# A transformer layer in fp32 on one core: the total of squares by one-column products

## The chip, the cores and the metric

The kernel runs on one core of a Trainium2 chip. The metric is the device time of one execution in microseconds (us), as the median of several runs. Before the change it is 652.82 us (three runs, 652.47 to 654.33).

## The reference

The input is x, 8 x 1024 tokens of 256 channels. First comes an attention block without a score matrix (softmax of q over the head's 16 channels, softmax of k over the tokens, state = kᵀv), with a residual and a layer norm. Then comes the feed-forward block, which is where the change lies:

```
h = layer_norm(x, ln1_g, ln1_b)
h = h @ ternary_quant(w1).T + b1            # 256 -> 1024
h = gelu(h)
h = layer_norm(h, ln2_g, ln2_b)             # over the 1024 hidden channels
out = h @ ternary_quant(w2).T + b2          # 1024 -> 256
x = _layernorm(x + out)
```

The second layer norm needs, for each token, the mean of its 1024 hidden values and the mean of their squares. This kernel never forms the normalised h: it multiplies the gelu's output by the second weights, and corrects the product with mean and deviation afterwards.

## The kernel before

The program has two phases, one after the other: `attention_phase`, which writes its result to a scratch tensor in HBM, and `feed_forward_phase`. Each engine has its instructions in an order written out by hand, and semaphores tie the engines together.

The feed-forward takes 512 tokens a step (four groups of 128), so there are 16 steps, k = 0 to 15. In a step the hidden channels are cut into eight pieces m = 0 to 7 of 128. For each m:

- TensorE, `first(k, m)` (L1496): four products 128x512 into a bank of `hps`, hidden channels on the partitions and tokens along the columns.
- ScalarE (L1215, L1227, L1229): gelu in place in the bank, its square into `sq` in SBUF, and the rounded high part `a_hi`.
- VectorE, `act_low` (L1312): the low part `a_lo`, what the rounding left. Only then is the bank free.
- TensorE, `second(k, m)` (L1512): eight products 128x258 into `yps`, tokens on the partitions. Of the 258 columns two carry the sum of the hidden values.

The squares are added over m: six of the eight on GpSimd (`accp`, L1187), two on VectorE (`accd`, L1321), and VectorE adds the two (L1328). What `accd` then holds is 128 partitions by 512 tokens, and the total over the 128 partitions is still to be made. `sum_transposes` (L1458) turns it by four transposes, so that the tokens lie on the partitions, and `hidden_stats` (L1349) sums each token's 128 columns into `sums`. From it and the mean VectorE forms the variance (L1351, L1354, L1357), GpSimd takes the root (L1158), and the residual is added (L1373).

`hps` has only four banks, which the eight pieces, the two transposes of the input and the total share in turn. A product into a bank waits for whatever read the bank last (`bank_free`, which waits for `hi_ok` and `lo_ok` of an earlier piece). TensorE's order of one step is in the loop at the end of the listing: the total of step k-1 stands between `first(k, 3)` and `first(k, 4)`. On VectorE the order around it is `hidden_mean(k)` (L1334, which waits for the last product of the second layer), `centre_y` of two groups (L1341), `act_low(k + 1, 1)`, `act_low(k + 1, 2)`, `centre_y` of the other two, `ht_low`, `act_low(k + 1, 3)`, `hidden_stats(k)`, `norm_apply(k + 3)`. `ones`, a 128x128 tile of 1.0 from the attention phase, is also the weight of the totals in `weight_sums` (L819):

```
for h in range(2):
    last = nc.tensor.matmul(aps[:, 0, 0:1], ones[:], wabs[:, n, h:h + 1], start=(h == 0), stop=(h == 1))
```

`weight_sums` is called twice in the attention phase.

Of the kernel before, what the change touches and what calls it, by code (L numbers as in the profile page):

```python
# [27 lines left out]
ALU = mybir.AluOpType  # L28
ACT = mybir.ActivationFunctionType
AX_X = mybir.AxisListType.X  # L30

P = 128
# [15 lines left out]
def wait_for(eng, semaphore, count):  # L48

    if not isinstance(count, int) or count > 0:  # L50
        eng.wait_ge(semaphore, count)
# [976 lines left out]
def feed_forward_phase(nc, kept, x1_scratch, out):  # L1028

    NB, _, T, _ = x1_scratch.shape  # L1030
    FC, C = kept.t2.shape[1:]
    CH = C // P
    F = FC * P
    TB = 4
# [13 lines left out]
    with ExitStack() as ctx:  # L1048
        def sb(name, shape, dt=F32):
            return ctx.enter_context(nc.sbuf_tensor("ff_" + name, shape, dt))  # L1050

        def sem(name):
            return ctx.enter_context(nc.semaphore("ff_" + name))
# [10 lines left out]
        accp, accd = sb("accp", [P, TOK]), sb("accd", [P, TOK])  # L1064
        z = sb("z", [P, 2, TB, C])
        t1, t2, vecs, ident, wstep, bias1 = kept.t1, kept.t2, kept.vecs, kept.ident, kept.wstep, kept.bias1
        u_row, c_row = kept.ff_u, kept.ff_c
        w2 = sb("w2", [P, FC, C + 2], F32R)
        g_hi = sb("g_hi", [P, FC], F32R)
        flat, g_safe, g_all, g_inv, rho, sig = (sb(n, [P, FC]) for n in  # L1070
# [1 line left out]
        rs1 = sb("rs1", [P, TB])  # L1072
        bnZ, mvZ, veZ, rsZ = sb("bnZ", [P, TB, 6]), sb("mvZ", [P, TB, 2]), sb("veZ", [P, TB]), sb("rsZ", [P, TB])
        nmr = sb("nmr", [P, TB])
        sums = sb("sums", [P, TB])
        nmu = sb("nmu", [P, TB])
        msq = sb("msq", [P, TB])
        var = sb("var", [P, TB])
# [13 lines left out]
        h_mm, gelu_ok, hi_ok, lo_ok, sq_ok = (sem(s) for s in ("h_mm", "gelu_ok", "hi_ok", "lo_ok", "sq_ok"))  # L1092
        y_mm = sem("y_mm")
        sum_p, sum_d = sem("sum_p"), sem("sum_d")
        r_tr, r_sum, r_mean, r_sq, r_var, r_eps, r_rstd, r_gain = (
            sem(s) for s in ("r_tr", "r_sum", "r_mean", "r_sq", "r_var", "r_eps", "r_rstd", "r_gain"))
        yc_ok, z_ok, z_stat, z_var, z_eps, z_rstd, z_nmr, o_ok = (
            sem(s) for s in ("yc_ok", "z_ok", "z_stat", "z_var", "z_eps", "z_rstd", "z_nmr", "o_ok"))
        o_out = [sem(f"o_out{n}") for n in range(2)]
# [6 lines left out]
        def ring(k, m):  # L1106
            return hps[:, (USES * k + FIRST_AT[m]) % RING]

        def ht_bank(k, c):
            return hps[:, (USES * k + HT_AT[c]) % RING]  # L1110

        def sum_bank(k):
            return hps[:, (USES * k + SUM_AT) % RING]
# [154 lines left out]
        def _(dve):  # L1268
# [47 lines left out]
            def square_sum(k, m):  # L1316
                if not 0 <= k < NK:
                    return
                dve.wait_ge(sq_ok, FC * k + m + 1)
                wait_for(dve, r_tr, k)  # L1320
                nc.vector.tensor_tensor(accd[:], sq[:, m - 1], sq[:, m], ALU.add).then_inc(sum_d, 1)  # L1321

            def square_total(k):
# [21 lines left out]
            def hidden_stats(k):  # L1345
                if not 0 <= k < NK:
                    return
                dve.wait_ge(r_tr, k + 1)
                nc.vector.tensor_reduce(sums[:], sum_bank(k).rearrange("p (t n) -> p t n", n=P), AX_X, ALU.add  # L1349
                                        ).then_inc(r_sum, 1)  # L1350
                nc.vector.tensor_tensor(msq[:], nmu[:], nmu[:], ALU.mult).then_inc(r_sq, 1)  # L1351
                dve.wait_ge(r_sum, k + 1)
                dve.wait_ge(r_sq, k + 1)
                nc.vector.scalar_tensor_tensor(out=var[:], in0=sums[:], scalar=1.0 / F, in1=msq[:],  # L1354
                                               op0=ALU.mult, op1=ALU.subtract).then_inc(r_var, 1)
                dve.wait_ge(r_var, k + 1)
                nc.vector.tensor_scalar(var[:], var[:], 0.0, EPS, ALU.max, ALU.add).then_inc(r_eps, 1)  # L1357
# [71 lines left out]
        @block.tensor  # L1429
        def _(pe):  # L1430
            def bank_free(k, m):
                pe.wait_ge(hi_ok, FC * k + m + 1)
                pe.wait_ge(lo_ok, FC * k + m + 1)

            def transposes(k, c):
                if not 0 <= k < NK:
                    return
                pe.wait_ge(n_ok, TB * (k + 1))
                if c == 0:
                    if k >= 2:  # L1440
                        bank_free(k - 2, 4)
                else:
                    pe.wait_ge(ht_lo_ok, CH * k + 1)
                for t in range(TB):
                    last = nc.tensor.transpose(ht_bank(k, c)[:, t * P:(t + 1) * P], xn[:, t, c * P:(c + 1) * P],  # L1445
                                               ident[:])
                last.then_inc(ht_tr, 1)

            def sum_transposes(k):
                if not 0 <= k < NK:  # L1450
                    return
                pe.wait_ge(sum_d, D_ADDS * (k + 1))
                if k < NK - 1:
                    bank_free(k + 1, 1)
                else:
                    bank_free(k, 6)
                for t in range(TB):
                    last = nc.tensor.transpose(sum_bank(k)[:, t * P:(t + 1) * P], accd[:, t * P:(t + 1) * P],  # L1458
                                               ident[:])
                last.then_inc(r_tr, 1)  # L1460

            def first(k, m):
                if not 0 <= k < NK:
                    return
                if m == 0:
                    pe.wait_ge(ht_hi_ok, CH * (k + 1))
                    pe.wait_ge(ht_lo_ok, CH * (k + 1))
                    if k < 1:
                        pe.wait_ge(ht_lo_ok, CH * k + 2)
                    else:  # L1470
                        bank_free(k - 1, 5)
                elif m == 1:
                    if k >= 1:
                        bank_free(k - 1, 6)
                elif m == 2:
                    if k >= 1:
                        bank_free(k - 1, 7)
                elif m == 3:
                    bank_free(k, 0)
                elif m == 4:  # L1480
                    bank_free(k, 2)
                elif m == 5:
                    if k < NK - 1:
                        pe.wait_ge(ht_lo_ok, CH * (k + 1) + 2)
                    else:
                        bank_free(k - 1, 4)
                elif m == 6:
                    bank_free(k, 3)
                elif m == 7:
                    if k < 1:  # L1490
                        bank_free(k, 1)
                    else:
                        pe.wait_ge(r_sum, k)
                for c in range(CH):
                    for j, h in enumerate((ht_hi, ht_lo)):
                        mm = nc.tensor.matmul(ring(k, m), t1[:, c, m * P:(m + 1) * P], h[:, k % 2, c],  # L1496
                                              start=(c == 0 and j == 0), stop=(c == CH - 1 and j == 1))
                mm.then_inc(h_mm, 1)

            def second(k, m):  # L1500
                if not 0 <= k < NK:
                    return
                if k == 0 and m == 0:
                    pe.wait_ge(w2_ok, FC)
                    pe.wait_ge(s_ok, 2)
                pe.wait_ge(hi_ok, FC * k + m + 1)
                pe.wait_ge(lo_ok, FC * k + m + 1)
                for t in range(TB):
                    if m == 0:
                        wait_for(pe, yc_ok, TB * (k - 1) + t + 1)  # L1510
                    for j, a in enumerate((a_hi, a_lo)):
                        last = nc.tensor.matmul(yps[:, t, 0:C + 2], a[:, m % DEPTH, t * P:(t + 1) * P], w2[:, m],  # L1512
                                                start=(m == 0 and j == 0), stop=(m == FC - 1 and j == 1))
                last.then_inc(y_mm, 1)

            for k in range(-2, NK + 1):
                second(k - 1, 5)
                first(k, 1)
                first(k, 2)
                second(k - 1, 6)  # L1520
                second(k - 1, 7)
                transposes(k + 1, 1)
                first(k, 3)
                sum_transposes(k - 1)
                first(k, 4)
                second(k, 0)
                first(k, 5)
                first(k, 6)
                second(k, 1)
                first(k, 7)  # L1530
                second(k, 2)
                second(k, 3)
                transposes(k + 2, 0)
                first(k + 1, 0)
                second(k, 4)
# [55 lines left out]
```

## Time and profile before

| | |
|---|---|
| median of three runs | 652.82 us |
| the profiled execution | 650.70 us |
| its span in the profile | 648.7 us |
| feed-forward, steady steps | about 376 to 620 us of the span |
| TensorE products busy | 556.7 us (86%) |
| VectorE busy | 521.0 us (80%) |
| ScalarE busy | 481.4 us (74%) |
| GpSimd busy | 426.0 us (66%) |

The profile is of one execution. Its times are us from the start of the span unless marked ns. PE is TensorE's products and PEld its weight loads, DVE is VectorE, ACT ScalarE, POOL GpSimd. "L1458" is line 1458 of the kernel, and out<-in names the tiles. PEclk is the clock that TensorE was granted, as a share of its full 2.4 GHz.

### The profile page before, as it was taken

How to read it: one execution, taken by the hardware profiler on the slowest of the kernel's cores; microseconds unless marked ns; L12 is line 12 of the kernel's file. 1: busy time of each engine (PE TensorE's matmuls, PEld its weight loads, DVE VectorE, ACT ScalarE, POOL GpSimd, SP SyncE). 2: the span in 40 equal slices, each digit the busy share in tenths (PEclk: the TensorE clock that was granted, in tenths of full speed). 3: DMA queues.
4: the chain of work that ended last, by engine and by line, in shares of the span. 5: the costliest groups of instructions: out<-in, count | busy, mean ns of one | idle time of the engine just before them, and what ended most of it. 6: DMA issues, size and time to landing. Idle time of an engine off the chain costs nothing. (4 is left out here: it accounts for less than half of the span.)

```text
span 648.7 us, 10895 instructions
## 1 busy us (share of the span) xinstructions
PE 556.7 (86%) x3584; PEld 500.7 (77%) x3584; DVE 521.0 (80%) x1308; ACT 481.4 (74%) x906; POOL 426.0 (66%) x414
## 2 busy tenths in 40 slices
PE   2789999889998999976805899999999999999981
PEld 2679899879987989776804788888888888888870
DVE  3995898988989797876423689999998989999875
ACT  1262677576856756756264988999999999999983
POOL 0287898879798898774122557766666666666661
PEclk9799999989999999998865999999999999999996
DMA  7311022060404021200032000222111122200002
GB/s 285 145 65 66 2 90 107 21 239 2 196 1 169 27 92 40 99 33 30 37 116 111 33 34 1 65 66 66 64 41 48 47 66 66 67 33 33 34 34 97
DMA packets 10711, 46.52 MB, mean 72 GB/s; under 512 B 1312, under 2 KB 1568, under 8 KB 8352
## 3 DMA queue, kind: packets, MB, share of 16 engines
q1 hardware_dynamic: 10656, 45.83, 19.3%
q8 instruction: 29, 0.48, 0.3%
q14 instruction: 26, 0.21, 0.1%
HBM read 29.02 MB, written 16.81 MB: 71 GB/s over the span
## 5 line engine op out<-in xcount | busy, mean ns | idle before, releaser
L1512 PE MATMUL yps<-ff_w,ff_a_hi 128*128 128x258 f32 x512 | 126.0, 282 | 0.9 <-DVE ff_a_lo L1312 0.7
L1512 PE MATMUL yps<-ff_w,ff_a_lo 128*128 128x258 f32 x512 | 125.9, 282 | 0.0
L1496 PE MATMUL hps<-ff_ht_hi,t 128*128 128x512 f32 x256 | 106.6, 416 | 3.1 <-DVE ff_a_lo L1312 2.7
L1312 DVE SCALAR_TENSOR_TENSOR ff_a_lo<-hps,ff_rho,ff_a_hi 128x512 fp32r<-128x512 f32 x128 | 93.9, 743 | 14.8 <-ACT ff_a_hi L1229 12.6
L1215 ACT ACTIVATE hps<-hps,bias,wstep 128x512 f32<-128x512 f32 x128 | 95.3, 772 | 9.5 <-PE hps L1496 8.7
L1496 PE MATMUL hps<-ff_ht_lo,t 128*128 128x512 f32 x256 | 102.3, 400 | 0.0
L1512 PEld LDWEIGHTS yps<-ff_w,ff_a_hi 128*128 128x128 f32 x512 | 96.9, 189 | 4.7 <-ACT ff_a_hi L1229 0.9
L1512 PEld LDWEIGHTS yps<-ff_w,ff_a_lo 128*128 128x128 f32 x512 | 96.6, 189 | 3.3
L1229 ACT ACTIVATE ff_a_hi<-hps,ff_rho 128x512 fp32r<-128x512 f32 x128 | 92.0, 719 | 0.0
L1187 POOL TENSOR_TENSOR ff_accp<-ff_accp,ff_sq 128x512 f32<-128x512 f32 x64 | 83.0, 1297 | 7.1 <-ACT ff_sq L1227 3.5
L1227 ACT ACTIVATE ff_sq<-hps 128x512 f32<-128x512 f32 x128 | 79.3, 620 | 0.1
L1174 POOL TENSOR_TENSOR ff_x1c<-ff_x,ff_c_row 128x512 f32<-128x512 f32 x32 | 38.1, 1189 | 44.8 <-DVE ff_z L1373 44.8
L1496 PEld LDWEIGHTS hps<-ff_ht_hi,t 128*128 128x128 f32 x256 | 49.0, 191 | 14.7 <-issue 4.2
L940 PE MATMUL aps<-r_hi,pt_hi 128*128 128x384 f32 x128 | 47.5, 371 | 12.0 <-DVE r_lo L510 6.6
L1496 PEld LDWEIGHTS hps<-ff_ht_lo,t 128*128 128x128 f32 x256 | 49.2, 192 | 7.6
L411 ACT COPY z<-aps 128x256 f32<-128x256 f32 x64 | 23.5, 382 | 36.5 <-DVE bnA L684 36.4
L280 POOL TENSOR_TENSOR xt_lo_then_t<-xt,xt_hi 128x1024 fp32r<-128x1024 f32 x16 | 39.4, 2464 | 16.7 <-ACT xt_hi L380 16.7
L684 DVE BATCH_NORM_STATS2 bnA<-aps 128x6 f32<-128x256 f32 x64 | 26.9, 427 | 26.4 <-PE aps L940 26.2
L271 POOL TENSOR_TENSOR xc_lo<-xc,xc_hi 128x1024 fp32r<-128x1024 f32 x14 | 33.5, 2394 | 18.7 <-ACT xc_hi L373 18.7
L940 PE MATMUL aps<-r_hi,pt_lo 128*128 128x384 f32 x128 | 43.8, 342 | 0.0
L940 PE MATMUL aps<-r_lo,pt_hi 128*128 128x384 f32 x128 | 43.7, 342 | 0.0
L1241 ACT ACTIVATE ff_z<-ff_z,ff_nmr,ff_rsZ 128x256 f32<-128x256 f32 x64 | 35.1, 613 | 9.2 <-DVE ff_nmr L1399 9.2
(185 smaller groups left out, 1708.8 us busy)
## 6 DMA issues: line engine op xcount, KB each, us to landing
x_scratch<-z SPq DMA_DIRECT2D x16, 514.0 KB, 2.8
ff_x<-x_scratch SPq DMA_DIRECT2D x16, 514.0 KB, 5.2
xc<-in_x_chan_dram SPq DMA_DIRECT2D x8, 1024.0 KB, 6.6
xt<-in_x_tok_dram SPq DMA_DIRECT2D x8, 1024.0 KB, 4.9
out_dram<-ff_z SPq DMA_DIRECT2D x16, 512.0 KB, 3.3
w_raw<-in_w_dram SPq DMA_DIRECT2D x2, 1024.0 KB, 4.7
rows<-in_rows_dram SPq DMA_DIRECT2D x1, 512.0 KB, 4.2
w_raw<-in_wq_dram SPq DMA_DIRECT2D x1, 256.0 KB, 2.7
```

The source lines that it names most:

```text
L271: nc.gpsimd.tensor_tensor(xc_lo[:, b % 2, c], xc[:, c], xc_hi[:, b % 2, c].bitcast(F32), ALU.subtract).then_inc(xc_lo_ok, 1)
L280: nc.gpsimd.tensor_tensor(xt_lo[:, ts], xt[:, b % 2, ts], xt_hi[:, ts].bitcast(F32), ALU.subtract).then_inc(xt_lo_ok, 1)
L940: last = nc.tensor.matmul(out, l, r, start=(c == 0 and k == 0), stop=(c == CH - 1 and k == 2), skip_group_check=True)
L1174: nc.gpsimd.tensor_tensor(x1c[:, k % 2, ts], x1[:, k % XB, ts, 0:C], c_row[:].rearrange("p (o c) -> p o c", o=1).to_broadcast([P, n, C]), ...
L1187: nc.gpsimd.tensor_tensor(accp[:], a, sq[:, m], ALU.add).then_inc(sum_p, 1)
L1215: nc.scalar.activation(ring(k, m), ring(k, m), ACT.Gelu, bias=bias1[:, m:m + 1], scale=wstep[:, 0:1]).then_inc(gelu_ok, 1)
L1227: nc.scalar.activation(sq[:, m], ring(k, m), ACT.Square).then_inc(sq_ok, 1)
L1229: nc.scalar.activation(a_hi[:, m % DEPTH], ring(k, m), ACT.Copy, scale=rho[:, m:m + 1]).then_inc(hi_ok, 1)
L1241: nc.scalar.activation(z[:, k % 2, t], z[:, k % 2, t], ACT.Identity, bias=nmr[:, t:t + 1], scale=rsZ[:, t:t + 1]).then_inc(o_ok, 1)
L1312: nc.vector.scalar_tensor_tensor(out=a_lo[:, m % DEPTH], in0=ring(k, m), scalar=rho[:, m:m + 1], in1=a_hi[:, m % DEPTH].bitcast(F32), op0= ...
L1496: mm = nc.tensor.matmul(ring(k, m), t1[:, c, m * P:(m + 1) * P], h[:, k % 2, c], start=(c == 0 and j == 0), stop=(c == CH - 1 and j == 1))
L1512: last = nc.tensor.matmul(yps[:, t, 0:C + 2], a[:, m % DEPTH, t * P:(t + 1) * P], w2[:, m], start=(m == 0 and j == 0), stop=(m == FC - 1 a ...
```

## The change

The total over the 128 partitions is made by TensorE itself. In place of a transpose, each 128x128 piece of `accd` becomes the weights of an fp32 product whose moving operand is one column of ones; the result is one column with the tokens on the partitions. Four such products fill four columns of the bank. VectorE's reduction and the tile `sums` go, and the variance's first step reads the four columns in the bank. `first(k, 7)`, which takes the same bank next, waits for that step (`r_var`) in place of the reduction (`r_sum`).

```diff
-        sums = sb("sums", [P, TB])
...
-                wait_for(dve, r_tr, k)
+                wait_for(dve, r_mm, k)
                 nc.vector.tensor_tensor(accd[:], sq[:, m - 1], sq[:, m], ALU.add).then_inc(sum_d, 1)
...
             def hidden_stats(k):
-                dve.wait_ge(r_tr, k + 1)
-                nc.vector.tensor_reduce(sums[:], sum_bank(k).rearrange("p (t n) -> p t n", n=P), AX_X, ALU.add
-                                        ).then_inc(r_sum, 1)
+                dve.wait_ge(r_mm, k + 1)
                 nc.vector.tensor_tensor(msq[:], nmu[:], nmu[:], ALU.mult).then_inc(r_sq, 1)
-                dve.wait_ge(r_sum, k + 1)
                 dve.wait_ge(r_sq, k + 1)
-                nc.vector.scalar_tensor_tensor(out=var[:], in0=sums[:], scalar=1.0 / F, in1=msq[:],
+                nc.vector.scalar_tensor_tensor(out=var[:], in0=sum_bank(k)[:, 0:TB], scalar=1.0 / F, in1=msq[:],
                                                op0=ALU.mult, op1=ALU.subtract).then_inc(r_var, 1)
...
-            def sum_transposes(k):
+            def sum_columns(k):
...
                 for t in range(TB):
-                    last = nc.tensor.transpose(sum_bank(k)[:, t * P:(t + 1) * P], accd[:, t * P:(t + 1) * P],
-                                               ident[:])
-                last.then_inc(r_tr, 1)
+                    last = nc.tensor.matmul(sum_bank(k)[:, t:t + 1], accd[:, t * P:(t + 1) * P], ones[:, 0:1],
+                                            start=(t == 0), stop=True, skip_group_check=True)
+                last.then_inc(r_mm, 1)
...
-                        pe.wait_ge(r_sum, k)
+                        pe.wait_ge(r_var, k)
```

TensorE's order before, at the total in a steady step, with the semaphores that each instruction waits for:

```order
L1496 MATMUL hps<-ff_ht_lo,t 128x512
L1458 MATMUL hps<-ident,ff_accd 128x128 [waits ff_lo_ok,ff_hi_ok,ff_sum_d]
L1458 MATMUL hps<-ident,ff_accd 128x128 x3
L1496 MATMUL hps<-ff_ht_hi,t 128x512 [waits ff_lo_ok,ff_hi_ok]
L1496 MATMUL hps<-ff_ht_lo,t 128x512
```

The same place now; the lines' numbers are four lower in the changed kernel:

```order
L1492 MATMUL hps<-ff_ht_lo,t 128x512
L1454 MATMUL hps<-ones,ff_accd 128x1 [waits ff_lo_ok,ff_hi_ok,ff_sum_d]
L1454 MATMUL hps<-ones,ff_accd 128x1 x3
L1492 MATMUL hps<-ff_ht_hi,t 128x512 [waits ff_lo_ok,ff_hi_ok]
L1492 MATMUL hps<-ff_ht_lo,t 128x512
```

Four instructions stand in the place of four; the waits before and behind them are the same. VectorE's order before, from the last `act_low` ahead of the statistics:

```order
L1312 SCALAR_TENSOR_TENSOR ff_a_lo<-hps,ff_rho,ff_a_hi 128x512 [waits ff_hi_ok]
L1349 TENSOR_REDUCE ff_sums<-hps 128x4 [waits ff_r_tr]
L1351 TENSOR_TENSOR ff_msq<-ff_nmu 128x4
L1354 SCALAR_TENSOR_TENSOR ff_var<-ff_sums,ff_msq 128x4 [waits ff_r_sq,ff_r_sum]
L1357 TENSOR_SCALAR ff_var<-ff_var 128x4 [waits ff_r_var]
```

And now:

```order
L1311 SCALAR_TENSOR_TENSOR ff_a_lo<-hps,ff_rho,ff_a_hi 128x512 [waits ff_hi_ok]
L1348 TENSOR_TENSOR ff_msq<-ff_nmu 128x4 [waits ff_r_mm]
L1350 SCALAR_TENSOR_TENSOR ff_var<-hps,ff_msq 128x4 [waits ff_r_sq]
L1353 TENSOR_SCALAR ff_var<-ff_var 128x4 [waits ff_r_var]
```

The reduction is gone, and the wait for TensorE's total is now the small square's.

## Rows read from the trace of the kernel before

**Rows 1.** The page: busy us, share of the span, instructions of each engine.
```profile
PE 556.7 (86%) x3584; PEld 500.7 (77%) x3584; DVE 521.0 (80%) x1308; ACT 481.4 (74%) x906; POOL 426.0 (66%) x414
```

**Rows 2.** The chain of waits over a step: start us, us, what.
```profile
444.02 0.18 DVE ff_nmu L1334
...
444.22 0.87 DVE ff_yc L1341 x2
445.10 0.68 DVE ff_a_lo L1312
445.77 0.14 issue
445.91 0.63 PE hps L1458 x4
...
446.56 1.17 PE hps L1496 x4
...
461.47 0.18 DVE ff_nmu L1334
```

**Rows 3.** Waits, 376 to 620 us: who, for whom: us, times, longest.
```profile
DVE ff_nmu L1334 <- PE yps L1512: 16.5, 14, 1.3
...
PEld hps L1458 <- issue: 13.3, 14, 1.0
...
PE hps L1458 <- DVE ff_a_lo L1312: 7.7, 14, 0.6
...
PEld hps L1496 <- issue: 3.9, 15, 0.6
```

**Rows 4.** Timeline of ScalarE, same step: start us, us, instruction [idle before].
```profile
449.66 0.75 ACT L1215 ACTIVATE hps<-hps,bias,wstep 128x512 f32<-128x512 f32 x1 [0.23 <-PE hps L1496]
```

**Rows 5.** Timeline of the weight loads, same step.
```profile
445.88 0.42 PEld L1458 LDWEIGHTS hps<-ident,ff_accd 128*128 128x128 f32 x4 [0.96 <-issue]
446.53 0.19 PEld L1496 LDWEIGHTS hps<-ff_ht_hi,t 128*128 128x128 f32 x1 [0.24 <-issue]
```

**Rows 6.** Timeline of VectorE, same step.
```profile
445.01 1.40 DVE L1312 SCALAR_TENSOR_TENSOR ff_a_lo<-hps,ff_rho,ff_a_hi 128x512 fp32r<-128x512 f32 x2
...
448.51 0.68 DVE L1349 TENSOR_REDUCE ff_sums<-hps 128x4 f32<-128x512 f32 x1
449.11 0.15 DVE L1351 TENSOR_TENSOR ff_msq<-ff_nmu 128x4 f32<-128x4 f32 x1
449.38 0.16 DVE L1354 SCALAR_TENSOR_TENSOR ff_var<-ff_sums,ff_msq 128x4 f32<-128x4 f32 x1
```

**Rows 7.** All instructions of line 1458: ns min/median/max, first and last start us.
```profile
L1458 PEld LDWEIGHTS hps<-ident,ff_accd x64: 137/141/143, 376.1 to 634.0; 128*128 128x128 f32 x64
```

**Rows 8.** Line 819: its loads, then its two places in the loads' timeline.
```profile
L819 PEld LDWEIGHTS aps<-wabs,ones x8: 188/190/192, 88.4 to 161.6; 128*128 128x128 f32 x8
...
88.45 0.53 PEld L819 LDWEIGHTS aps<-wabs,ones 128*128 128x128 f32 x4
88.90 0.19 PEld L882 LDWEIGHTS ring<-xc_hi,w_hi 128*128 128x128 f32 x1
...
161.30 0.53 PEld L819 LDWEIGHTS aps<-wabs,ones 128*128 128x128 f32 x4
...
161.75 0.19 PEld L882 LDWEIGHTS ring<-xc_hi,w_hi 128*128 128x128 f32 x1
```

**Rows 9.** Timeline of TensorE, same step: the first product of m = 7.
```profile
451.36 0.39 PE L1496 MATMUL hps<-ff_ht_hi,t 128*128 128x512 f32 x1
```

**Rows 10.** The end: chain of waits, then the last total in TensorE's timeline.
```profile
635.87 0.60 DVE ff_sums L1349
...
636.65 0.17 DVE ff_var L1354
...
633.82 0.60 PE L1458 MATMUL hps<-ident,ff_accd 128*128 128x128 f32 x4
```

**Rows 11.** Windows: stretch, its us, busy us (instructions) of each engine, PEclk, DMA share, GB/s.
```profile
345.00:360.00 15.00, 9.09 (x31) 6.99 (x32) 5.74 (x11) 9.71 (x16) 5.39 (x5) 0.66 0.01 3
...
376.00:634.00 258.00, 248.21 (x1590) 219.11 (x1591) 232.27 (x590) 248.74 (x434) 170.32 (x144) 1.00 0.15 48
```

More of the change, by code:

```diff
@@ L1066, in feed_forward_phase @@
         t1, t2, vecs, ident, wstep, bias1 = kept.t1, kept.t2, kept.vecs, kept.ident, kept.wstep, kept.bias1
-        u_row, c_row = kept.ff_u, kept.ff_c
+        u_row, c_row, ones = kept.ff_u, kept.ff_c, kept.ones
         w2 = sb("w2", [P, FC, C + 2], F32R)
@@ L1094, in feed_forward_phase @@
         sum_p, sum_d = sem("sum_p"), sem("sum_d")
-        r_tr, r_sum, r_mean, r_sq, r_var, r_eps, r_rstd, r_gain = (
-            sem(s) for s in ("r_tr", "r_sum", "r_mean", "r_sq", "r_var", "r_eps", "r_rstd", "r_gain"))
+        r_mm, r_mean, r_sq, r_var, r_eps, r_rstd, r_gain = (
+            sem(s) for s in ("r_mm", "r_mean", "r_sq", "r_var", "r_eps", "r_rstd", "r_gain"))
         yc_ok, z_ok, z_stat, z_var, z_eps, z_rstd, z_nmr, o_ok = (
@@ L1523, in _ @@
                 first(k, 3)
-                sum_transposes(k - 1)
+                sum_columns(k - 1)
                 first(k, 4)
```

## The prediction, made before the changed kernel was run

> **What bounds the kernel now.** I read the busy times first. TensorE has the most work but no engine is full, so shares don't decide [rows 1]. The chain of waits comes next, over one step of the feed-forward: it repeats every 17.45 us (444.02 to 461.47), and in it TensorE runs without a break except in one place [rows 2]. There the last product of the second layer lets VectorE form the mean (0.18 us), centre two quarters of y (0.87) and write ff_a_lo (0.68), 0.14 us pass until TensorE sees it, and then the four transposes start at 445.91. The table of waits says the same over the whole stretch: VectorE waits 16.5 us for TensorE before that mean in 14 steps (about 1.2 us each), and TensorE waits 7.7 us for ff_a_lo before the transposes in 14 steps (0.55 each) [rows 3]. So VectorE is on the path only between the end of the second layer and ff_a_lo; the rest of its step, the sum along 512 columns included, ends early and is followed by its own idle time. ScalarE is the next fullest: it works nearly without a break too, but what little it idles is a wait for TensorE (0.23 us) [rows 4], so it follows when TensorE moves.
>
> One more wait is easy to miss. The transposes' weight loads begin at 445.88 and the group takes 0.42 us, until 446.30; but the next load (m = 4 of the first layer) begins only at 446.53, and the profile calls these 0.24 us "issue" [rows 5]. That product waits for lo_ok of m = 2 (`bank_free(k, 2)`), the second of the two ff_a_lo in the VectorE row that starts at 445.01 and lasts 1.40, so it ends at 446.41 [rows 6]; 0.12 us later is 446.53, the delay seen at the first ff_a_lo. The waits show it in 15 steps, 3.9 us in all [rows 3]. From the first load of the group, TensorE thus has 0.65 us (445.88 to 446.53) that VectorE's second ff_a_lo fills anyway, and the transposes use 0.42 of them.
>
> **The change, part by part.**
>
> VectorE loses a reduction of 680 ns in each of 16 steps. It starts at 448.51, and the variance starts 0.87 us later at 449.38 [rows 6]; by issue times the reduction holds the queue for 0.60 us (448.51 to the small square that now takes its place). What follows it on VectorE then runs 0.60 us sooner: normalising the next tokens, statistics, further ff_a_lo. TensorE waits for none of these between 446.56 and the end of the second layer, since there is no gap there [rows 2]. So in the 15 steps that have a successor, this is worth nothing: it lengthens a wait of 1.25 us that is already there. The price of the cover going is likewise nothing, as the cover is TensorE itself.
>
> TensorE loses four transposes (64 weight loads over 16 steps, so one record per instruction [rows 7]) and gets four fp32 products with one column. The shape is in the trace already: line 819 forms a total with ones as the weights and one column passing. The program has four such instructions and the profile shows eight loads and eight products, two records for each [rows 8]. Per step the change therefore issues eight loads and eight short products. The weights are now the 128 x 128 piece of accd, and the ones pass: loads of full width as in line 819. Its loads start at 88.45 and the next foreign load at 88.90, after four records; the second time at 161.30 and 161.75: 0.45 us / 4 = 0.1125 us per record, twice alike [rows 8]. Eight cost 0.90 us. The load of m = 4 then starts at 445.88 + 0.90 = 446.78, in place of 446.53: **+0.25 us** per step. Only that much, since 0.65 us of the 0.90 lie beside ff_a_lo.
>
> The bounds of this term. Line 819 runs behind dense work and has four records; here there are eight, they follow an idle stretch, and each takes other weights. Below: the four transposes' own spacing, (0.42 - 0.14)/3 = 0.093 us with 0.14 us as the length of one load [rows 5, 7], gives 0.75 us, +0.10 a step. Above: 0.12 us, a little over line 819's spacing by the rounding of two starts and a slower start from rest (the 0.03 us between load and product after the wait), gives 0.96 us, +0.31 a step. I take 0.1125, the row of the very shape.
>
> The same place weighed against the Trainium skill. The row gives 0.1125 us per load with its short product [rows 8]. "TensorE: Matmul & The Clock Gate", section "Back-to-back issue gap", has about 81 ns per pair of load and product in a sustained stream of 128-column products, and a floor of about 25 ns for very small products taken alone. By the first figure eight would be an estimated 0.65 us and by the floor 0.20; either would fit into the wait, and the sum would be -0.6 us in place of +3.2. I go by the row.
>
> Moved waits. The first layer's m = 7 now waits for the variance's first step (r_var) in place of the reduction. Even in the old profile that step is formed by 449.38 + 0.16 = 449.54, and m = 7 starts at 451.36, 1.8 us later [rows 6, 9]; now both the square and the variance come 0.60 us sooner against the VectorE work ahead of them, and TensorE is 0.25 us later. No cost. The variance reads four columns of the bank directly in place of sums; the products end at about 447 and the read comes after 448.5, so nothing waits. The two waits that open the total (sum_d, and lo_ok of m = 1) are as before. The semaphore and the small tile that go cost nothing.
>
> The end. Behind the last step there is no TensorE work to hide VectorE: the chain of the end goes through the reduction (635.87, 0.60 us) and the variance (636.65) [rows 10], and on through the root on GpSimd, the residual and the last output, all one behind the other. There the removal counts in full: **-0.60 us**. The last total's products come behind the last of the second layer, at 633.82; eight records end them near 634.8, and VectorE comes to them at 635.8, so their cost is covered by 1 us.
>
> **Sum.** 15 steps x 0.25 = +3.75; end -0.60; together **+3.15 us**. The profiled execution took 650.70 us (span 648.7 and 2.0 around it), so it would be 653.85. It lies 2.1 us under the median of the runs shown, 652.82; the same step on that median gives **655.97**, which I give as 656.0. With the bounds: 15 x 0.10 - 0.6 = +0.9, and 15 x 0.31 - 0.6 = +4.05, so 653.7 to 656.9.
>
> **Rivals.**
>
> A, the new group fits into the wait. If loads and short products follow each other at 0.65 us / 8 = 0.081 us or less, the group is over by 446.53, when ff_a_lo frees the next product anyway. Then no step changes and only the end's -0.60 remains: 652.2, no change that can be told. For it: the transposes come to 0.093 with 128 columns each, so shorter products might space closer. Against it: line 819 has 0.1125 with a single column, twice. 10%.
>
> B, VectorE's time counts in every step (the other side). If VectorE came late to the mean, each of the 16 steps would give back 0.60 us: 652.82 - 9.6 = 643.2. It decides from the point where VectorE's idle time before the mean is nil. The trace has 1.25 us there [rows 3]. I leave 3%, also for a part of it through contention that less VectorE work might ease.
>
> C, the loads don't overlap the short products. At the 0.19 us that one load of this kind lasts [rows 8], eight take 1.52 us, +0.87 a step, +13.05 - 0.6: 665.3. For it: a start from rest, with changing weights. Against it: the spacing in line 819 is well below the length of one of its loads. 4%.
>
> D, TensorE's clock falls. It is granted in full (1.00) through 376 to 634 us although TensorE rests once a step, and was at 0.66 when it had work for only 9.09 of 15 us [rows 11]. The total now leaves the array nearly empty for 0.9 us behind a pause of 0.55. Were the next 3 us of each step done at 1.2 GHz, each would cost 3 us more: +45 us, near 697. Against it: the resting stretch grows only from 1.2 to 1.45 us. 2%.
>
> **How the numbers follow.** The forecast has 81%. A measurement of this kernel can tell 0.3% (2.0 us) from no change. In the forecast's case +3.15 is slower; its lower bound would count as no change, for which I take 5% off it. Slower: 76 + 4 + 2 = 82%. Same: 10 + 5 = 15%. Faster: 3%. The range: from 653.6, a tenth under the forecast's lower bound, to 656.9 plus 1.3 us for the spread of the runs before (652.47 to 654.33) and a partly slower group: 658.2. A, B, C and D stay outside, some 19%.
>
> **What would show it.** The total's group has eight loads a step (128 in all), and from its first load to that of m = 4 are 0.90 us. The idle time called issue ahead of m = 4 (0.24) is gone. The period is 17.70 us. VectorE's wait before the mean grows from 1.25 to 1.25 + 0.60 + 0.25 = 2.10 us, and TensorE's 0.55 before the total stays. The clock stays at 1.00. At the end the variance follows the centred y at once. If the period is 17.45, A holds; if VectorE's idle time doesn't grow by the reduction, I misread who waits; a period above 18 means C or D, told apart by the clock.

## The result, and the profile after

The changed kernel takes 657.92 us (median of 12 runs, 655.45 to 662.43), beside 653.01 us for the kernel before (12 runs, 646.51 to 662.03). The ratio is 1.0085 (95% interval 1.0055 to 1.0115). By the ratio the change costs 5.5 us, where the forecast was 3.15; the two medians lie 4.9 apart. The ratios use the fast runs alone, which leaves out one run of the kernel before here, and five of the changed kernel's twelve in the first of the later comparisons. Two later comparisons of the very same two kernels gave 1.0033 (0.9983 to 1.0083) and 1.0036 (1.0004 to 1.0068). All three intervals hold 1.006, and that is also what the traces come to below.

The page of the changed kernel, which answers to [rows 1]: VectorE has lost 7.5 us of work, TensorE has gained 8.3 us of products and 11.3 us of weight loads.

```profile
PE 565.0 (86%) x3648; PEld 512.0 (78%) x3648; DVE 513.5 (78%) x1292; ACT 481.8 (73%) x906; POOL 426.1 (65%) x414
```

The chain of waits over a step (start us, us, what) answers to [rows 2]. Its members are the same, and only the total has grown:

```profile
449.40 0.18 DVE ff_nmu L1333
...
449.60 0.87 DVE ff_yc L1340 x2
450.47 0.67 DVE ff_a_lo L1311
451.14 0.14 issue
451.28 1.02 PE hps L1454 x8
452.30 1.04 PE hps L1492 x4
...
467.06 0.18 DVE ff_nmu L1333
```

The period is 17.66 us (449.40 to 467.06) in place of 17.45. The timeline of the weight loads at that place, beside [rows 5]:

```profile
451.25 0.97 PEld L1454 LDWEIGHTS hps<-ones,ff_accd 128*128 128x128 f32 x8 [0.95 <-issue]
452.14 0.19 PEld L1492 LDWEIGHTS hps<-ff_ht_hi,t 128*128 128x128 f32 x1
```

Eight loads, and from the first to that of m = 4 are 0.89 us, in place of 0.65; the 0.24 us of "issue" ahead of m = 4 is gone. The table of waits (who, for whom: us in total, times, longest), beside [rows 3]:

```profile
DVE ff_nmu L1333 <- PE yps L1508: 16.9, 14, 2.1
DVE ff_a_lo L1311 <- ACT ff_a_hi L1228: 13.8, 15, 1.9
PEld hps L1454 <- issue: 13.3, 14, 1.0
...
PE hps L1454 <- DVE ff_a_lo L1311: 7.7, 14, 0.6
```

TensorE waits for VectorE's first ff_a_lo as long as before. VectorE's wait before the mean has not grown (16.9 us, 16.5 before). What VectorE was spared stands in the second row: it now waits for ScalarE's high part further down the step. The same row of the kernel before was small:

```profile
DVE ff_a_lo L1312 <- ACT ff_a_hi L1229: 2.2, 3, 1.2
```

**Three stretches.** The start of the mean (L1334, now L1333) marks each step, so every profile can be cut in three stretches: up to the mean of step 0, from there to the mean of step 15, and from there to the end. All kernels run here are in the table; "falls" is explained below, and the ratio is that of each comparison against the kernel before, with its interval.

| kernel | to first mean | steps | usual step | falls | end | ratio |
|---|---|---|---|---|---|---|
| before | 374.2 | 259.8 | 17.45 | 0 | 14.70 | |
| before, again | 377.1 | 259.6 | 17.43 | 0 | 14.70 | 0.9997 (0.9961 to 1.0033) |
| before, a third time | 373.8 | 259.8 | 17.45 | 0 | 14.70 | 0.9992 (0.9960 to 1.0024) |
| changed | 378.7 | 263.4 | 17.67 | 0 | 14.02 | 1.0085 (1.0055 to 1.0115) |
| changed, again | 377.6 | 264.9 | 17.66 | 1 | 14.02 | 1.0033 (0.9983 to 1.0083) |
| changed, a third time | 373.7 | 264.7 | 17.67 | 1 | 14.02 | 1.0036 (1.0004 to 1.0068) |
| VectorE's half only | 376.8 | 260.8 | 17.45 | 0 | 14.02 | 0.9957 (0.9914 to 1.0000) |
| TensorE's half only | 375.5 | 264.9 | 17.66 | 1 | 14.69 | 1.0064 (1.0026 to 1.0102) |
| four fp32r products | 383.3 | 259.8 | 17.45 | 0 | 14.02 | 1.0013 (0.9985 to 1.0042) |
| 12 records | 377.2 | 281.8 | 18.11 | 8 | 14.02 | 1.0301 (1.0249 to 1.0352) |
| 16 records | 378.1 | 294.9 | 18.57 | 12 | 14.03 | 1.0507 (1.0465 to 1.0550) |
| 16 transposes | 373.2 | 275.2 | 18.47 | 0 | 14.69 | 1.0231 (1.0174 to 1.0288) |
| before, other VectorE order | 374.9 | 258.7 | 17.45 | 0 | 14.71 | 0.9980 (0.9952 to 1.0009) |
| changed, other VectorE order | 377.0 | 258.4 | 17.43 | 0 | 14.03 | 0.9973 (0.9942 to 1.0004) |

The first profiles of the two kernels differ by 7.4 us of span, and 4.5 of it lie ahead of the first mean, where the two kernels issue the same instructions. The table shows that stretch anywhere from 373.2 to 383.3 us, the three profiles of the kernel before among them with 373.8 to 377.1; the three of the changed kernel have 373.7 to 378.7. So I don't count it to the change. A part of its spread is the clock: ahead of the first mean TensorE was granted half its clock for 47.8 us in two of the profiles of the kernel before (374.2 and 373.8) and for 54.6 us in the third (377.1); in those of the changed kernel, for 54.6 us (378.7 and 377.6) and 47.8 us (373.7). The first pair compared 47.8 with 54.6 us.

### The profile page after: what moved, and what is told of

Read it like the earlier page. It is cut to its first block and busy times, and to the rows that moved or that the text cites. A ratio compares the mean times of both kernels' runs of the same rounds, so it can differ in the third digit from the quotient of the medians.

```text
span 656.1 us, 10991 instructions
## 1 busy us (share of the span) xinstructions
PE 565.0 (86%) x3648; PEld 512.0 (78%) x3648; DVE 513.5 (78%) x1292; ACT 481.8 (73%) x906; POOL 426.1 (65%) x414
```

## Experiments

**The two kernels again.** No edit. First the kernel before, then the changed one.

> The kernel before, unchanged, as a control. Theory T (the change costs 15 x 0.22 us in the steady steps and gives back 0.6 to 0.7 us at the end, +2.9 in all; the rest of the measured gap comes from the stretch ahead of the first mean of the feed-forward, where the instructions are the same and the granted clock differs from run to run): ratio 1.000, and its profile has steps of 17.45 us and a first mean some us away from 374.2. Rival R (the stretch ahead of the first mean is slower because of the change): first mean within 1 us of 374.2.

> The changed kernel, unchanged, as a control. Theory T: steps of 17.67 us again, mean of step 0 to mean of step 15 about 263.1 us, from the last mean to the end about 14.0; its first mean not tied to 378.7; ratio to before near 1.0045. Rival R: first mean again at about 378.7, ratio 1.008.

The control is at 1.000. Its first mean moved from 374.2 to 377.1 with the same program, as theory T says and rival R does not. (That of the changed kernel came at 377.6, and in a third profile at 373.7.) The changed kernel has its steps of 17.66 us again, but its steps come to 264.9 us, not 263.1: the last interval, from the mean of step 14 to that of step 15, took 17.31 us in place of 15.76. Windows around it (stretch, its us, busy us and instructions of each engine, granted clock, DMA share, GB/s):

```profile
625.00:628.20 3.20, 2.21 (x15) 1.71 (x14) 3.00 (x7) 3.17 (x7) 3.20 (x3) 1.00 0.00 0
628.20:631.60 3.40, 3.40 (x14) 2.96 (x14) 2.54 (x7) 1.68 (x3) 2.41 (x3) 0.53 0.40 157
631.60:636.00 4.40, 4.40 (x27) 3.91 (x26) 1.47 (x9) 3.42 (x6) 1.51 (x2) 0.98 0.00 0
```

For 3.4 us TensorE is granted 1.2 GHz, half its clock, and then the full clock again. The timeline shows what it did before:

```profile
627.05 1.02 PE L1454 MATMUL hps<-ones,ff_accd 128*128 128x1 f32 x8 [0.99 <-DVE ff_a_lo L1311]
627.94 0.47 PE L1492 MATMUL hps<-ff_ht_hi,t 128*128 128x512 f32 x1
628.25 0.50 PE L1492 MATMUL hps<-ff_ht_lo,t 128*128 128x512 f32 x1
628.55 0.63 PE L1492 MATMUL hps<-ff_ht_hi,t 128*128 128x512 f32 x1
```

It rested 0.99 us (the last full step's rest is longer than the usual 0.55), did the total's one-column products, and from the third dense product on each took 0.63 us in place of 0.40, with the second in between (0.50). Such a stretch I call a fall; it costs 17.31 - 15.76 = 1.55 us.

**Each half alone.** VectorE's half: the transposes stay, the reduction goes.

```diff
-                nc.vector.tensor_reduce(sums[:], sum_bank(k).rearrange("p (t n) -> p t n", n=P), AX_X, ALU.add
-                                        ).then_inc(r_sum, 1)
...
-                dve.wait_ge(r_sum, k + 1)
...
-                nc.vector.scalar_tensor_tensor(out=var[:], in0=sums[:], scalar=1.0 / F, in1=msq[:],
+                nc.vector.scalar_tensor_tensor(out=var[:], in0=sum_bank(k)[:, 0:TB], scalar=1.0 / F, in1=msq[:],
...
-                        pe.wait_ge(r_sum, k)
+                        pe.wait_ge(r_var, k)
```

> Only VectorE's half of the change: the four transposes stay, the reduction over 512 columns is left out and the variance reads four columns of the bank (so the squares' total is left out of the result). Theory T: steps stay at 17.45 us, VectorE's wait before the mean grows from 1.25 to about 1.85, the end is 0.6 us shorter: -0.6 us, ratio 0.999. Rival (VectorE's time counts in every step): -9 us, steps of 16.85.

Steps of 17.45 us and an end of 14.02 in place of 14.70: VectorE's time counts at the end, 0.68 us, and nowhere else. One step took 18.46 us; its chain of waits holds 4.98 us of an output's DMA. The ratio, 0.9957, lies further down than these 0.68 us, but its interval reaches 1.0000 and holds them. As in the changed kernel, the wait before the mean did not grow, and a wait for ScalarE did:

```profile
DVE ff_nmu L1334 <- PE yps L1509: 15.8, 14, 2.1
...
DVE ff_a_lo L1312 <- ACT ff_a_hi L1229: 10.5, 15, 1.6
```

TensorE's half: the changed kernel with the reduction put back behind r_mm, into `sums`, which nobody reads.

```diff
+        sums = sb("sums", [P, TB])
...
                 dve.wait_ge(r_mm, k + 1)
+                nc.vector.tensor_reduce(sums[:], sum_bank(k).rearrange("p (t n) -> p t n", n=P), AX_X, ALU.add
+                                        ).then_inc(r_sum, 1)
                 nc.vector.tensor_tensor(msq[:], nmu[:], nmu[:], ALU.mult).then_inc(r_sq, 1)
+                dve.wait_ge(r_sum, k + 1)
```

> Only TensorE's half: one-column products as in the change, but VectorE still reduces 512 columns of the bank afterwards (over other data, so the total is wrong). Theory T: steps of 17.67 us, end as before: +3.3 us, ratio 1.005. Rival (contention with VectorE's reduction makes up part of the steps' price): steps differ from 17.67 by over 0.05.

The variance still took the columns, so the result was complete, other than the expectation says. Steps of 17.66 us: the whole price of a step is TensorE's, and VectorE's reduction has no part in it. The end is 14.69, as before. There is a fall again in the last full step, which the expectation did not have.

**Four loads in place of eight.** The sum is written as fp32r and multiplied by two fp32r columns of ones; such a product is one load and one product in the trace.

```diff
+        accr, ones_r = sb("accr", [P, TOK], F32R), sb("ones_r", [P, 2], F32R)
...
-                nc.vector.tensor_tensor(accd[:], accd[:], accp[:], ALU.add).then_inc(sum_d, 1)
+                nc.vector.tensor_tensor(accr[:], accd[:], accp[:], ALU.add).then_inc(sum_d, 1)
...
-                nc.vector.scalar_tensor_tensor(out=var[:], in0=sum_bank(k)[:, 0:TB], scalar=1.0 / F, in1=msq[:],
+                nc.vector.scalar_tensor_tensor(out=var[:], in0=sum_bank(k)[:, 0:2 * TB:2], scalar=1.0 / F, in1=msq[:],
...
+            nc.vector.tensor_copy(ones_r[:], ones[:, 0:2])
...
-                    last = nc.tensor.matmul(sum_bank(k)[:, t:t + 1], accd[:, t * P:(t + 1) * P], ones[:, 0:1],
+                    last = nc.tensor.matmul(sum_bank(k)[:, 2 * t:2 * t + 2], accr[:, t * P:(t + 1) * P], ones_r[:],
```

> The change with the total as rounded fp32 (fp32r) operands, two equal columns each: one load and one product for each instruction, four of each a step in place of eight. Theory T (eight loads of 0.11 us overrun the 0.65 us that the second ff_a_lo leaves; four take 0.44 and fit): steps of 17.45 us and 0.6 us less at the end: -0.6 us against before. Rival (the columns cost through something else than the number of loads, such as the fp32 form or the short product): steps stay at 17.6 or more.

```profile
454.97 0.52 PEld L1456 LDWEIGHTS hps<-ff_ones_r,ff_accr 128*128 128x128 f32 x4 [0.95 <-issue]
455.63 0.19 PEld L1494 LDWEIGHTS hps<-ff_ht_hi,t 128*128 128x128 f32 x1
```

The loads take 0.52 us, the next begins 0.66 us after the first, when VectorE's second ff_a_lo frees it, and the steps are back at 17.45. So what costs is the overrun of that wait, and it is the number of loads, each with its short product, that overruns it: they are 0.11 us apart in this form too. (Which of the two sets the 0.11 us isn't shown, as no kernel has one without the other.) The ratio, 1.0013 (0.9985 to 1.0042), is too wide to show the 0.6 us at the end; the end itself has them (14.02).

**More records.** Twelve: two of the four products done twice. Sixteen: all four.

```diff
+                for t in range(TB):      # range(2) in the kernel with 12 records
+                    nc.tensor.matmul(sum_bank(k)[:, 8 + t:9 + t], accd[:, t * P:(t + 1) * P], ones[:, 0:1],
+                                     start=(t == 0), stop=True, skip_group_check=True)
                 for t in range(TB):
                     last = nc.tensor.matmul(sum_bank(k)[:, t:t + 1], accd[:, t * P:(t + 1) * P], ones[:, 0:1],
```

> The change with the eight loads and products done twice (16 records a step, the second set into columns that nobody reads). Theory T: a further 8 x 0.11 = 0.88 us in each of 15 steps, so steps of 18.55 us, +13.2 over the changed kernel and about +16 over before. Rival (a fixed cost for turning to fp32 and back, with cheap loads): clearly under 0.88 a step.

> The changed kernel with two of the four one-column products done twice: 12 loads and products a step. Theory T2 (the steady price is 0.11 us per record beyond what fits; besides, TensorE's clock falls for some 3.4 us and costs 1.5 us whenever rest and one-column products together last too long): steps of 18.11 us without a fall (17.67 + 0.44), falls in more steps than with 8 records (none or one of 15) and in fewer than with 16 (11 of 14). Rival (only the loads count, and the falls at 16 are another matter): no falls, +9.5 us over before.

An undisturbed step takes 18.57 us with sixteen and 18.11 with twelve: 0.90 and 0.44 over 17.67, so 0.11 us a record. But of the 15 intervals, 12 with sixteen records and 8 with twelve are longer by 1.5 us more, each with a fall. The expectation for sixteen had none, and missed half of the +33 us. Nor do the lengths of rest and products alone decide where a fall comes, as theory T2 has it: with twelve records the last full step rests 0.99 us and has no fall, while eight of the 14 steps that rest 0.55 us have one. The chain of waits of a fall with sixteen records, where the dense products behind it take 1.53 and 2.83 us in place of 0.96 and 1.87:

```profile
400.00 1.02 PE hps L1454 x8
401.02 0.89 PE hps L1457 x8
401.92 1.03 PE hps L1495 x4
402.95 1.53 PE yps L1511 x8
404.48 2.83 PE hps L1495 x8
```

And the granted clock in windows of it:

```profile
398.30:402.00 3.70, 3.15 (x24) 2.66 (x22) 3.68 (x8) 3.25 (x6) 3.42 (x4) 1.00 0.00 0
402.80:406.20 3.40, 3.40 (x14) 3.01 (x13) 2.05 (x8) 0.75 (x1) 1.06 (x1) 0.54 0.00 0
```

**The same time in transposes.** To tell the time between dense products from what fills it, the kernel before does its four transposes four times over: `for t in (0, 1, 2, 3) * 4:`.

> The kernel before with the four transposes of the total done four times over: 16 transposes of 128 columns a step, about as long as 16 one-column records (16 x 0.11 = 1.76 us), after the same rest. If the clock falls because the array is nearly empty in one-column products: few falls, steps of about 18.6 us, low-clock time as in the kernel before (60 to 62 us a run). If it is the transposes' form or mere time between dense products that counts: falls in most steps as with 16 one-column records, low-clock time near 100 us, about +33 us.

Steps of 18.47 us, so the detour is nearly as long as with sixteen one-column records (18.57), behind the same rest. Not one fall:

```profile
409.00:427.50 18.50, 17.95 (x122) 16.21 (x122) 15.87 (x41) 17.31 (x31) 11.90 (x10) 1.00 0.19 58
```

So it isn't the time without dense products alone: what fills it counts, and here one-column products lose the clock in most steps where transposes don't. Whether the rest ahead of them is needed too isn't shown; no kernel here has sixteen one-column records without it. The Trainium skill, "TensorE: Matmul & The Clock Gate", section "Part 4: PE-mode transpose", says that the full clock doesn't engage for transposes, which don't count as busy in the same way. The trace does not agree: sixteen of them a step, among dense products, kept it at 1.00 where sixteen one-column records lost it.

The mean clock of every single run tells much the same without a look at its trace. At half clock for a time L, the mean is lowered so that L = 2 x span x (1 - mean clock). Averaged over a kernel's runs:

| kernel | L, us |
|---|---|
| before, in five sets of 11 to 29 runs | 59.9 to 61.9 |
| VectorE's half only | 61.0 |
| changed, three sets | 64.5, 64.7, 64.5 |
| TensorE's half only | 65.3 |
| 12 records | 87.8 |
| 16 records | 100.9 |
| 16 transposes | 58.0 |
| four fp32r products | 62.5 |
| other VectorE order, before and changed | 61.3, 62.0 |

With 3.4 us for one fall, 8 falls give 61 + 27 = 88 and 12 give 61 + 41 = 102, as measured. The changed kernel's 3 to 4 us fit about one fall a run, but that is near what the method can tell: the runs of one kernel scatter by 3 to 5 us (standard deviation), and the fp32r kernel, whose profile has no fall, stands at 62.5.

**The third pair of profiles.**

> The changed kernel once more, for the count of falls. Theory T2: steps of 17.67 us but for those with a fall (+1.5 us), most likely the last full one, where TensorE rests 0.99 us in place of 0.55; low-clock time 3 us above the kernel before; ratio about 1.006.

> The kernel before once more beside it: low-clock time of 60 to 62 us a run, steps of 17.45, no fall in the last full step, ratio 1.000.

The changed kernel had its fall where expected (a last interval of 17.33 us), behind a rest of 0.98 us:

```profile
623.01 1.02 PE L1454 MATMUL hps<-ones,ff_accd 128*128 128x1 f32 x8 [0.98 <-DVE ff_a_lo L1311]
623.90 0.67 PE L1492 MATMUL hps<-ff_ht_hi,t 128*128 128x512 f32 x1
624.37 0.63 PE L1492 MATMUL hps<-ff_ht_lo,t 128*128 128x512 f32 x1
```

The kernel before rests there just as long, does four transposes (in 0.63 us), and keeps the clock; its last interval is 15.53:

```profile
619.89 0.63 PE L1458 MATMUL hps<-ident,ff_accd 128*128 128x128 f32 x4 [0.99 <-DVE ff_a_lo L1312]
620.55 0.47 PE L1496 MATMUL hps<-ff_ht_hi,t 128*128 128x512 f32 x1
620.86 0.39 PE L1496 MATMUL hps<-ff_ht_lo,t 128*128 128x512 f32 x1
```

**Another order on VectorE**, on both kernels:

```diff
                 hidden_mean(k)
-                centre_y(k, (0, 1))
                 act_low(k + 1, 1)
                 act_low(k + 1, 2)
+                centre_y(k, (0, 1))
                 centre_y(k, (2, 3))
```

> The kernel before with another order on VectorE: behind the mean both ff_a_lo (m = 1 and 2 of the next step), and only then the centring of all four groups of y. Theory T says the load of m = 4 waits for the second ff_a_lo alone, and that one can start once ScalarE's high part is there (1.3 us after the mean starts): it would end 0.3 us sooner, steps of 17.1 to 17.2, -4 us. Rival: second(k, 0) then waits for the centred y, and the steps stay at 17.45 or grow.

> The changed kernel with that same order on VectorE. Theory T: the total's products start 0.87 us sooner, when ff_a_lo of m = 1 is done, and run beside the second ff_a_lo; eight loads end about when that one does: steps of 17.1 to 17.2 us, -4.5 us against before and -7.5 against the changed kernel. Rival: the centred y comes too late for the second layer's m = 0 and takes it back.

Steps of 17.1 us came, but only the first two; all others took 17.45 and 17.43. Windows over 395 to 600 us, first of the kernel before and then of the changed one, both in this order:

```profile
395.00:600.00 205.00, 200.82 (x1272) 175.67 (x1271) 186.56 (x486) 201.22 (x352) 137.18 (x117) 1.00 0.16 52
```

```profile
395.00:600.00 205.00, 204.89 (x1319) 182.12 (x1318) 181.00 (x475) 200.85 (x353) 139.02 (x117) 1.00 0.17 52
```

ScalarE is busy for 98% in both, and in the changed kernel TensorE for 99.9%. In the first, the chain of waits of a step now runs for its greater part through ScalarE's squares and high parts; an excerpt:

```profile
485.23 0.59 ACT ff_sq L1227
485.82 0.58 ACT ff_a_hi L1229
486.40 0.49 ACT ff_sq L1227
```

So my -4 us failed on the next engine. By the first window, TensorE works for 17.1 us of a 17.45 us step and ScalarE for 17.1 too. In what is left, TensorE waits for an ff_a_lo, which needs ScalarE's high part, and ScalarE waits for TensorE (395 to 600 us):

```profile
PE hps L1496 <- DVE ff_a_lo L1312: 4.1, 11, 0.4
ACT hps L1215 <- PE hps L1496: 3.7, 12, 0.9
```

ScalarE was as full in the old order (200.73 us of the same 205), so a change on VectorE alone had next to nothing to gain. That the first two steps are shorter for want of the output's normalisation on ScalarE fits the order of the program; it wasn't tried. The second rival fell: TensorE has no wait for the centred y in either. The useful part is that in this order the eight records cost nothing, as they fill what TensorE idled: the steps come to 258.4 us against 258.7, and the end keeps its 0.68 us. At 0.9973 (0.9942 to 1.0004) it is the fastest of the kernels with a complete result, but can't be told from the kernel before.

## Why the prediction was right or wrong

- **What bounds the kernel, and the hidden wait.** Right for this change. TensorE's chain sets the step, and the second ff_a_lo covers 0.65 us of the total; four loads fit into it (17.45), eight don't. That ScalarE merely follows held by a margin of some 0.3 us a step, as the other order showed.
- **Price of a record and of a step.** Right, and nearly exact: 0.89 us for the eight, and +0.22 a step (17.67), where I had 0.90 and +0.25 [rows 8].
- **VectorE's time in the steps.** Worth nothing, as forecast. But I had it lengthen the wait before the mean to 2.10 us; that stayed at 1.2 us, and the time went into waits for ScalarE. I had looked for the idle time where it was, not where it would arise.
- **The end.** -0.60 forecast, -0.68 measured (14.70 to 14.02).
- **The clock: this step failed.** I wrote "The clock stays at 1.00", rival D took a fall as something that comes in every step or never, at 2%, and the sum had no term for it. It comes once a run where it comes, in the last full step, where the rest is 0.99 us and not 0.55: in two of three profiles of the changed kernel, and in that of TensorE's half. It costs 1.55 us, half as much as the forecast's whole sum. What decides whether it comes stays open.
- **The sum.** Averaged over the three profiles of each, the steps grow from 259.7 to 264.4 us, +4.6, and the end shrinks by 0.7: **+3.9 us**, 0.6%, against my +3.15. In it are 15 x 0.22 = 3.3 us, two thirds of a fall (1.0), and in two of three profiles one step that is 0.3 us longer; in the first, that step's chain holds a wait for the output's DMA:

```profile
613.19 4.42 DMA out_dram<-ff_z
```

- **The measured 5.5 us.** The median of 657.92 lies in the range, and the direction was right; but the ratio, put on the 652.82 us that the forecast started from, gives 658.4, just above the range's end of 658.2. The fall doesn't account for that: the profile of this comparison has none. Its 7.4 us of span are 3.6 in the steps, -0.7 at the end, and 4.5 ahead of the first mean, with 54.6 us at half clock there against 47.8. At the 1.55 us that 3.4 us at half clock cost in the steps, I estimate 3.1 of the 4.5 us for that difference. The first comparison's interval reaches down to 3.6 us, and the two later ones (2.2 and 2.4 us) lie on the other side of 3.9, so the spread of runs can make up the rest. I had set 1.3 us aside for it in the range, from three runs that lay within 1.9 us, and nothing in the time itself; twelve runs of the kernel before lie between 646.51 and 662.03. That the time came into the range by its median is partly luck.
- **Rivals.** A fell with the eight loads' 0.89 us. B fell with VectorE's half alone. C fell with 0.11 us a record. D's mechanism came, but once a run at 1.55 us and not 15 times at 3; with sixteen records it came in 12 of 15 intervals.

## What to carry to other kernels

Moving a reduction to TensorE is paid in weight loads with their short products, here two of each for an fp32 product and one for an fp32r product. So price it by their number and ask how many of them fit beside a wait that is there anyway. Look for the place where the product behind is held by something else, as with the second ff_a_lo here: up to it loads are free, beyond it they count in full. And where TensorE has rested, what it does next matters: sixteen one-column records with rests of mostly 0.55 us ahead of them brought its clock down in 12 of 15 intervals, sixteen transposes of nearly the same length (1.70 us in place of 1.78) in none. Before taking time from one engine, see how full the next one is: ScalarE had 0.3 us a step left, and the other order on VectorE, meant to save 0.3 us a step, ended there.

## What the runs showed of the hardware

- Eight one-column fp32 records behind 0.55 us of rest: in the three profiles of the changed kernel, no fall in 42 usual steps; behind 0.99 us of rest, two falls in three, and one in TensorE's half. Twelve records: 8 falls in 15 intervals, none of them in the last full step with its 0.99 us of rest. Sixteen: 12 in 15. Sixteen transposes: none in 15.
- Each fall is a stretch of 3.4 us at 1.2 GHz and costs 1.5 us among dense products.
- The spacing of one-column records is 0.11 us whether four, eight, twelve or sixteen follow each other, and also right after a rest. Sixteen transposes have 0.106 us.
- Ahead of the first mean, where the kernels of the table issue the same instructions (the fp32r kernel has one more), the time at half clock goes from 44.4 us (16 transposes, first mean at 373.2) to 58.0 us (fp32r, 383.3). Left open: why it differs between executions, and what makes up the rest of the 10 us.
